# Fused cross attention and mixture of experts: VectorE's two products of a head pair moved behind the splits of keys

## The reference

```python
# x: 2 x 1024 x 256; ctx: 2 x 64 x 256; 8 heads of 64
def xattn(x, latents, mask, ...):            # called with x = ctx, latents = layernorm(x)
    q = latents @ Wq
    k, v = split(concat([x, latents]) @ Wkv)
    q, k = l2norm(q) * q_scale, l2norm(k) * k_scale
    attn = softmax(where(mask, q @ k.T * 8, -inf))
    return layer_norm((attn @ v) @ Wo)
def ffn(x, ...):                             # a shared expert of 1024 units, 16 routed of 256, two a token
    gates = top2(sigmoid(x @ router_w) + expert_bias)
    return swiglu(x, shared) + sum(gate * swiglu(x, expert))
x = x + xattn(...)
x = x + ffn(layernorm(x))
```

## Time and profile before

| | |
|---|---|
| median of 3 runs | 808.24 us (808.1 to 809.76) |
| profiled execution | 810.73 us, of which the span from first to last instruction is 808.6 us |
| PE, DVE, ACT, POOL busy | 98%, 62%, 42%, 42% of the span |
| granted TensorE clock, mean | 0.998 of full |
| projections | up to about 80 us |
| attention, pairs 0 to 7 | about 100 to 475 us, of which a pair takes 44 to 49 us |
| shared expert, first part, and routing | to 616 us |
| slots of the routed experts | to 753 us |
| shared expert, last part, combines | to 808.6 us |

### The profile page before, as it was taken

One profiled execution on the slowest core, in us unless ns is written; L12 is line 12 of the kernel. 1 busy time (PEld: TensorE's weight loads), 2 busy tenths in 40 slices (PEclk: granted clock), 3 DMA queues, 4 the chain that ended last, 5 costly groups with the idle time before them and its releaser, 6 DMA issues.

```text
span 808.6 us, 13028 instructions
## 1 busy us (share of the span) xinstructions
PE 789.2 (98%) x4358; PEld 483.3 (60%) x4359; DVE 500.9 (62%) x918; ACT 341.8 (42%) x643; POOL 341.1 (42%) x252
## 2 busy tenths in 40 slices
PE   8999999999999999999999998999999999999998
PEld 5444355454555545454554555756557999999655
DVE  4887777787787868787786755547212333333254
ACT  4555466665656566555665421131102333333110
POOL 2100055858585876855596233301661000000364
PEclk9999999999999999999999999999999999999999
DMA  3106700000000010000121102682522222222243
GB/s 118 41 26 202 227 2 1 3 26 1 29 1 28 1 28 2 12 16 1 28 66 28 27 26 79 196 269 82 189 91 66 92 91 91 91 91 84 80 143 116
DMA packets 52837, 56.39 MB, mean 70 GB/s; under 512 B 9258, under 2 KB 47668, under 8 KB 52788
## 3 DMA queue, kind: packets, MB, share of 16 engines
q1 hardware_dynamic: 49556, 47.23, 18.8%
q0 software_dynamic: 3072, 8.39, 3.2%
q10 hardware_dynamic: 160, 0.14, 0.0%
HBM read 36.73 MB, written 18.67 MB: 69 GB/s over the span
## 4 chain that ended last, share of the span: by engine, by line
PE 86%; issue 6%; DVE 3%; POOL 1%; ACT 1%; DMA 1%; POOLq 0%; DVEq 0%; SPq 0%; ACTq 0%
PE bank L1156 12%; PE bank L971 12%; PE bank L998 11%; PE bank L1221 10%; PE bank L845 10%; PE bank L1171 7%; PE bank L932 6%; PE bank L1230 5%; PE bank L976 4%; PE bank L916 2%; PE bank L1064 1%; PE bank L1211 1%; ACT prob L1341 1%; PE bank L1009 1%; DVE mx L1565 1%
## 5 line engine op out<-in xcount | busy, mean ns | idle before, releaser
L1341 ACT ACTIVATE prob<-bank,zero 128x512 f32<-128x512 f32 x256 | 160.9, 684 | 79.7 <-PE bank L976 77.5
L1565 DVE TENSOR_REDUCE mx<-bank 128x1 f32<-128x512 f32 x256 | 164.3, 685 | 47.7 <-PE bank L932 46.4
L732 POOL TENSOR_TENSOR acc<-acc,prob 128x1024 f32<-128x1024 f32 (+1 forms) x67 | 166.3, 2482 | 9.6
L998 PE MATMUL bank<-prob,vn 128*64 128x512 f32 x512 | 121.1, 602 | 0.0
L1156 PE MATMUL bank<-xfT,w12s 128*128 128x512 f32 x256 | 114.8, 593 | 0.8 <-ACT xfT L1402 0.8
L807 POOL DMA_INDIRECT slot_result<-slot_results,posi x32 | 31.1, 973 | 160.1 <-DMA slot_results<-yo 148.2
L1221 PE MATMUL bank<-xsT,w_slot 128*128 128x128 f32 x752 | 91.9, 275 | 1.0 <-ACT xsT L1436 1.0
L1221 PEld LDWEIGHTS bank<-xsT,w_slot 128*128 128x128 f32 x752 | 89.2, 191 | 6.0 <-ACT xsT L1436 1.6
L724 POOL TENSOR_TENSOR acc<-prob 128x1024 f32<-128x1024 f32 x16 | 40.6, 2534 | 122.1 <-ACT prob L1341 99.9
L1156 PEld LDWEIGHTS bank<-xfT,w12s 128*128 128x128 f32 x256 | 48.4, 190 | 49.7 <-issue 48.4
L1426 ACT ACTIVATE hidden_units<-bank 128x512 f32<-128x512 f32 x32 | 19.1, 597 | 130.0 <-PE bank L1156 130.0
(11 more groups left out here) (180 smaller groups left out, 1111.0 us busy)
## 6 DMA issues: line engine op xcount, KB each, us to landing
w12r<-in_L_ffn_routed_w SPq DMA_DIRECT2D x32, 256.0 KB, 4.0
slot_rows<-zrow SPq DMA_DIRECT2D x47, 128.0 KB, 1.9
xsl<-slot_rows SPq DMA_DIRECT2D x47, 128.0 KB, 2.0
slot_results<-yo SPq DMA_DIRECT2D x47, 128.0 KB, 1.7
w3r<-in_L_ffn_routed_w SPq DMA_DIRECT2D x16, 256.0 KB, 3.1
rec<-row_sum_reciprocals SPq DMA_DIRECT2D x30, 128.0 KB, 2.9
xin<-in_x SPq DMA_DIRECT2D x16, 128.0 KB, 2.1
w12s<-in_L_ffn_shared_w SPq DMA_DIRECT2D x2, 1024.0 KB, 8.5
```

The source lines that it names most:

```text
L732: g.tensor_tensor(acc[rows, c, :, :], acc[rows, c, :, :], prob[rows, n % PROBS, :, :], ALU.add).then_inc(summed, 1)
L998: last = mm_(o_bank(i, c)[rows, :], vn[:, kt, b, (2 * j + h) * DH:(2 * j + h + 1) * DH], prob[:, n % PROBS, h, :], start=(s == 0), stop=(s ...
L1341: a(prob[rows, held % PROBS, h, :], bank[2 * (n % 2) + h][rows, :], ACT.Exp, bias=bias[rows, :])\
L1565: v.tensor_reduce(mx[:, h, t, c:c + 1], ring_bank(u)[:, :], AX.X, ALU.max).then_inc(ring_used, 1)
```

## The change

1. In pairs 1 to 6 both `divide`s of the pair before stand together, behind the splits of `K_RIGHT` and `K_CTX`, at the end of the fourth phase. Before, the first stood ahead of these splits, and the second at the end of the fifth phase. Pair 7 keeps its order.
2. GpSimd waits, ahead of adding slot 13 (`BOTH + 5`), until VectorE's last `add_two` of the pair is done.
3. From `BREAK` on, `hidden` uses three pairs of banks in turn, waits for the product two steps back, and `down` follows two steps behind, so that three of them stand at the end.

```diff
     def hidden_pair(n):
-        if n < WIDE or n >= BREAK:
+        if n >= BREAK:
+            return (0, 1, 3)[(n - BREAK) % 3]
+        if n < WIDE:
             return n % 2
...
     def down_after(n):
...
         if n == SU * NG - 1:
-            return range(n - 1, n + 1)
-        if n in (0, WIDE, BREAK):
+            return range(n - 2, n + 1)
+        if n in (0, WIDE, BREAK, BREAK + 1):
             return ()
-        return (n - 2,) if WIDE < n < BREAK else (n - 1,)
+        return (n - 2,) if n > WIDE else (n - 1,)
...
             add_last(i, 0, LEFT_TAIL, LEFT_SUMMED)
-            for s in range(BOTH + 3, BOTH + 7):
-                add_more(i, 1, s)
+            add_more(i, 1, BOTH + 3)
+            add_more(i, 1, BOTH + 4)
+            pool.wait_ge(tail_ready, TAILS * (i + 1))
+            add_more(i, 1, BOTH + 5)
+            add_more(i, 1, BOTH + 6)
             add_last(i, 1, TAILS, SUMS)
...
-            elif WIDE < n < BREAK:
+            elif n > WIDE and n != BREAK:
                 pe.wait_ge(hid_ready, n - 2)
             else:
                 wait(pe, hid_ready, n - 1)
+            if n == BREAK + 2:
+                pe.wait_ge(yo_ready, NS)
...
                         if not more:
                             add_left()
-                        if i:
+                        if i and not more:
                             divide(2 * i - 2)
                     for one in place_rounds(i, f, a):
                         reduce_round(*one)
                     for turn in place_turns(i, f, a):
                         split_heads(*turn)
+                    if f == 3 and a == BATCH and i and more:
+                        divide(2 * i - 2)
+                        divide(2 * i - 1)
...
-                if f == 4 and more and i:
-                    divide(2 * i - 1)
```

## The result

| | before | after |
|---|---|---|
| median | 808.95 us (808.1 to 809.76, 4 runs) | 834.76 us (832.68 to 835.99, 4 runs) |
| profiled execution | 810.73 us, span 808.6 | 835.77 us, span 833.6 |
| mean granted TensorE clock | 0.998 | 0.981 |

The ratio is 1.0315, with a 95% interval of 1.029 to 1.0339: 3% slower. The forecast was 828 us and slower, in a range of 806 to 832. The sign and the mechanism came out as forecast, and the time lies 2.8 us above the range.

What follows compares the result with a forecast made beforehand. TensorE, busy 98% of the span, was taken to bound the kernel. Added to the 808.24 us median, +26.4 (products) - 4.3 (pair 5) - 4.0 (edit 2) + 2.1 (edit 3) = +20.2 gave 828 us, range 806 to 832.

Steps and rivals of the forecast that it cites:

- Steps (b) to (d): In pairs 1 to 6, GpSimd's add goes between the two products, the reduction is late, TensorE stands 3.0 us.
- The first rival: VectorE keeps its turn from the first divide to the second, so the kernel is not slower: 807 us; chance 0.25.
- Pair 5's 4.3 us: In the attention, a GpSimd add delayed this pair's first divide; moving the products takes the 4.3 us away.
- Step (e): Lower TensorE clock after each standstill in pairs 1 to 6 costs 1.4 us a pair, bounds 0 and twice that.
- Edit 2: In the attention, add_two takes 1.22 us and TensorE's wait for neg_max goes: 0.8 us five times, -4.0 us.
- Edit 3: In the last stage, second combine and gathers come 3.4 us later; the end moves by +2.1 us, bounds 0 and 3.4.
- The near tie: In pairs 1 and 5 before, GpSimd's add and VectorE's first divide start 0.02 us apart; GpSimd, then VectorE, stood.

Runs made afterwards that it cites:

- e5_add_waits_both: Kernel before with edit 1 alone, plus GpSimd's add of the context slot waiting until both products are done: 815.62 us, ratio 1.0023.
- e10_whole_with_wait: The whole change plus GpSimd's add of the context slot waiting until both products are done: 817.16 us, ratio 1.0044 against the kernel before.
- the first group: First of three groups of follow-up runs, each sharing one chip and its runs of the kernel before; here that kernel's median was 808.44 us.
- e3_last: Kernel before with edit 3 alone, the last stage's three pairs of banks and later down: 810.37 us, ratio 1.002.
- e3b_last: Kernel before with edit 3 alone, run a second time, in the third group: 816.65 us, ratio 1.0036.
- e7_combines_first: Kernel before with edit 3 alone, and the combines of step 24 ahead of add_shared(2) instead of behind it: 813.66 us, ratio 1.0002.
- e7b_combines_first: Second run of edit 3 with the combines of step 24 ahead of add_shared(2), against the kernel before: 814.01 us, ratio 0.9996.
- e8_products_adds: Kernel before with edits 1 and 2, without edit 3: 835.88 us, ratio 1.0275.
- e4_one_behind: Kernel before with only the first product behind the splits, the second still at the fifth phase's end, edits 2 and 3 left out: 821.6 us, ratio 1.0154.
- e1_products: Kernel before with edit 1 alone, both products behind the splits: 829.78 us, ratio 1.0251.
- e9_three_orders: Kernel before with only the first product behind the splits, edit 2, and GpSimd's slot 11 add waiting for both products: 810.27 us, ratio 0.9957.
- the second and third group: Follow-up runs, each group sharing one chip and its runs of the kernel before; that kernel's medians were 813.28 and 813.70 us.
- e6_ordered: Kernel before with edit 2, and GpSimd's first add of the right half waiting until the first product is done: 807.65 us, ratio 0.9932.

## Why the prediction was right in kind and short in size

- **Steps (b) to (d), the turn between the products**: right, to 0.1 us. Forecast were 177.41 and 180.2 for the ends of the products, 180.1 for the reduction, 3.0 us of standstill. The trace has 180.18, 180.10, and 17.9 / 6 = 3.0 us. All 18 pairs 1 to 6 of the three profiles with this order (the whole change, edit 1, edits 1 and 2) have it, and holding GpSimd back (`e5_add_waits_both`, `e10_whole_with_wait`) takes it away. By the rule of the Trainium skill (SBUF — State Buffer, "Who interferes with whom") that issue order decides who blocks, the add goes ahead of the second product; the trace agrees: the add stands from 177.01, the second product from 177.34, and the add ends first, at 179.63. The first rival, that VectorE keeps its turn between neighbours, is excluded.
- **Pair 5's 4.3 us in the sum: the step that failed, a term taken off the wrong base.** It was right for the profiled execution and wrong for the median. In the 17 executions of before in the first group the ten with a clock of 1.000 have spans of 805.2 to 807.2 us, and the others, at 0.998 or 0.999, reach 807.2 to 809.7. Four profiled executions leave the attention as before (`e3_last`, `e3b_last`, `e7_combines_first`, `e7b_combines_first`), with six first products each: of the 24, one has the collision (2.88 us, in pair 1 of `e7_combines_first`), and the other 23 take 0.68 us. I took 4.3 us off for a collision that, by these clocks and profiles, most executions don't have, and then added the rest to the median. An execution without it has six waits for `neg_max` and not five (`e3_last`: 3.9 us, 6), so that edit 2 is worth 6 x 0.8 = 4.8. The sum on the right base is 808.24 + 26.4 - 4.8 + 2.1 = 831.9, that is 3.5 us more than the forecast.
- **Step (e), the clock: a term that was sized too small.** I took 1.4 us a pair from the one case before. TensorE's busy time in a pair is 44.02 us in edit 2 alone, at full clock. In the changed kernel it is 45.3 in four pairs, 1.3 more, and 46.6 in two, 2.6 more. In sum the six pairs took 293.3 us, against 264.9 for edit 2 alone. That is 28.4 more, 17.9 of it standstill and 10.5 the clock's; forecast were 26.4 and 8.4. I had named 0 to 2.8 a pair as bounds, and then gave them no width in the range: 6 x 1.4 more would have been 8 us.
- **The two together** give 831.9 + 2.0 = 833.9 us, against 834.76 measured and 832 as the end of the range. Either alone would have left the time inside it: 831.9 with the base put right, 828.4 + 2.0 = 830.4 with the clock.
- **Edit 2**: right alone (4.8 us, forecast 4.0). Inside the whole change its gain is not its own, since with edit 1 VectorE comes to `add_two` when GpSimd's adds have ended; the sum for the whole stays the same.
- **Edit 3**: 2.1 us forecast, 2.1 in the trace, 1.6 and 2.9 alone. The shift of the gather (3.4 us forecast, 3.43 measured) is as worked out. TensorE's wait of 1.1 us ahead of the last `down`, for a product late behind the combines, was not in it; it is hidden by the combines.
- **Not forecast**: 1.9 us between the attention and the last stage (307.3 us instead of 305.4 from the last reciprocal to the begin of the last stage). There a wait of 2.2 us, 1.8 before, was followed by a clock of 0.64. The other profiles show that this comes and goes with the execution, and not with the change. `e7b_combines_first`, with the attention of before, has it too (a wait of 2.1 us, 307.4 us, and the line below), and `e7_combines_first`, the same kernel, has not (1.1 us, 304.9). Nor do edits 1 and 2 (`e8_products_adds`: 1.1 us, 304.7) or the whole change with its added wait (1.0 us, 304.6).

```profile
499.00:503.00 4.00, 4.00 (x11) 2.76 (x11) 3.49 (x11) 0.60 (x1) 1.98 (x3) 0.58 0.00 0
```

The profile difference adds up: 22.7 us from `add_two` to `add_two` over pairs 1 to 6 (293.3 - 270.6), -1.0 ahead of them (the five profiles with the attention of before differ by up to 2.3 us there, so this is not shown to be the change's), -0.7 behind, where a wait for `neg_max` is gone, +1.9 and +2.1: 25.0 us, which is 833.6 - 808.6.

## What to carry to other kernels

Before moving a VectorE instruction with two SBUF inputs, look not only at what waits behind it but at which GpSimd instruction will stand ready when it ends; two such instructions in a row gave a GpSimd add that stood ready a place between them, and cost the length of that add. A semaphore that holds GpSimd back for 1 to 2 us a pair was worth 5 us here (edit 2) and 18 to 22 (the line of `e5_add_waits_both` and `e10_whole_with_wait`); and an engine freed early must be followed to its next collision, as `e4_one_behind` shows. The fastest version is edit 2 alone, with or without the tie settled: ratio 0.9932.

When a term comes from one event in one profiled execution, ask whether the executions in the median have it before it is added to the median, and let the bounds of a cost that occurs six times stand six times in the range.

## What the hardware showed that I had not expected

The same standstill is not always followed by a lower clock. In `e7_combines_first` the near tie went to GpSimd in pair 1, TensorE stood for 1.75 us as in pair 5 of before, and the clock stayed at full:

```profile
179.08 0.50 PE L934 MATMUL bank<-k_hi,q_hi 64*128 64x512 f32 x2 [1.75 <-DVE k_lo L1555]
```

```profile
178.00:181.00 3.00, 1.92 (x15) 1.41 (x17) 2.36 (x6) 0.97 (x2) 2.86 (x2) 1.00 0.00 0
```

Between the attention and the last stage, standstills of 2.0 and 2.1 us left the clock at full (`e3_last`, `e5_add_waits_both`, `e3b_last`), and others of 2.1 and 2.2 us were followed by 0.57 to 0.64 over 4 us (`e7b_combines_first`, `e1_products`, the changed kernel). Behind standstills of 2.9 to 3.2 us it fell in every one of the 18 pairs; TensorE's busy time grew by 1.1 to 1.4 us in 14 of them and by 2.4 to 2.6 in four. What decides between these was not tried.

One VectorE instruction with a single SBUF tensor as input is held as well: `zneg` (8 elements a partition, multiplied by -1) took 0.17 us in pair 1 of the changed kernel with GpSimd idle, and in `e9_three_orders` 0.68 with GpSimd's adds under way: it ended at 190.17, right behind their end at 190.14. The reduction `mm` just ahead of it, as small, took 0.18 us in both, so its size is not the reason. What is was not tried.

ScalarE's standstill of 10.7 to 15.7 us in the last stage came in all eight profiles of the second and third group, and in none of the six others, whose longest wait there is 4.56 us. With the last stage as before it took 59.8 to 59.9 us (`e5_add_waits_both`, `e6_ordered`, `e8_products_adds`) and 58.6 (`e9_three_orders`), and 55.1 to 55.2 in the profiles without it. That may be why the kernel before is some 5 us slower in these two groups, but it was not profiled there. The trace names TensorE's bank as the end of the standstill in these four and only something remote in the other four. Its cause stays open.
